# A graph attention layer: edge tiles taken two at a time, one PSUM sum and one addition per pair

## The reference, cut to what is computed

```python
xh = (x @ W).reshape(N, H, D)                       # N x 8 x 32
a_src, a_dst = einsum(xh, att_src), einsum(xh, att_dst)   # N x 8
e = leaky_relu(a_src[src] + a_dst[dst], 0.2)
m = segment_max(e, dst, N)
e = exp(e - m[dst])
denom = segment_sum(e, dst, N)
msg = xh[src] * (e / denom[dst])[:, :, None]
out = segment_sum(msg, dst, N) + bias               # then batch norm, + x
```

## Time and profile before

| | |
|---|---|
| median of 3 runs | 2181.05 us (2179.94 to 2183.12) |
| the profiled execution | 2179.96 us |
| its span, first to last instruction | 2178.0 us |
| busy: PE, PE weight loads | 1758.3 us (81%), 1227.8 us (56%) |
| busy: DVE, ACT, POOL | 1415.2 us (65%), 1108.1 us (51%), 1214.5 us (56%) |
| mean granted TensorE clock | 0.908 |
| edge gathers | 879, 838.9 us of POOL |

### The profile page before, as it was taken

The page is one execution under the profiler, slowest core; times in us unless marked ns, Lnnn a source line. Parts: engine busy times, 40 slices in busy tenths (PEclk is TensorE's granted clock), DMA queues, the critical chain, the costliest instruction groups (busy, mean ns, idle before and its releaser), DMA issues. The chain is left out here.

```text
span 2178.0 us, 37746 instructions
## 1 busy us (share of the span) xinstructions
PE 1758.3 (81%) x10860; PEld 1227.8 (56%) x10860; DVE 1415.2 (65%) x3855; ACT 1108.1 (51%) x2386; POOL 1214.5 (56%) x1142
## 2 busy tenths in 40 slices
PE   7567778678777687687776887788399999999997
PEld 5334445354444354454443444447179999999996
DVE  6745666567666566566665676589956666666664
ACT  4444655465556456455654565548644444444443
POOL 1465655566656556566655566642046666656653
PEclk9778988888989889889998899899699999999999
DMA  8543444443444344344533444426723333333322
GB/s 292 168 123 95 123 108 116 116 136 97 121 138 123 96 130 126 97 125 122 146 93 108 133 127 108 118 61 229 292 64 51 51 51 51 50 51 51 51 43 36
DMA packets 124147, 240.42 MB, mean 110 GB/s; under 512 B 25064, under 2 KB 82996, under 8 KB 122772
## 3 DMA queue, kind: packets, MB, share of 16 engines
q0 software_dynamic: 62800, 147.76, 28.7%
q1 hardware_dynamic: 51816, 80.51, 11.2%
q10 hardware_dynamic: 9340, 9.73, 1.3%
HBM read 195.47 MB, written 43.30 MB: 110 GB/s over the span
## 5 line engine op out<-in xcount | busy, mean ns | idle before, releaser
L1145 POOL DMA_INDIRECT gather_ring<-node_table,src_slot x879 | 838.9, 954 | 530.8 <-issue 238.8
L1273 PE MATMUL bank<-gather_ring,onehot 128*128 128x264 f32 x1758 | 622.6, 439 | 262.0 <-DVE gather_ring L1197 222.0
L1239 PE MATMUL bank<-ones 128*128 128x512 bf16 x1803 | 595.0, 412 | 50.9 <-ACT gather_ring L1315 31.6
L1273 PEld LDWEIGHTS bank<-gather_ring,onehot 128*128 128x128 f32 x1758 | 340.2, 214 | 496.6 <-DVE gather_ring L1197 320.2
L1169 DVE TENSOR_TENSOR acc<-acc,bank 128x264 f32 x879 | 370.9, 422 | 192.5 <-remote 98.7
L1197 DVE TENSOR_TENSOR gather_ring<-gather_ring,bank 128x256 f32<-128x256 f32 x879 | 361.6, 412 | 0.3 <-ACT bank L1314 0.3
L1314 ACT ACTIVATE bank<-zbuf 128x64 f32<-128x64 f32 x110 | 25.0, 228 | 615.2 <-DVE zbuf L1191 346.5
L2240 POOL DMA_INDIRECT out_rows<-y,token_idx x105 | 203.6, 1939 | 218.4 <-DMA out_rows<-y,token_idx 151.7
L1239 PEld LDWEIGHTS bank<-ones 128*128 128x128 bf16 x1803 | 180.5, 104 | 208.4 <-issue 81.1
L2148 PE MATMUL bank<-xe,w_hi 128*128 128x256 f16 (+1 forms) x1792 | 284.2, 267 | 3.8 <-DVE xe L2070 2.6
L2208 ACT ACTIVATE hid<-bank,cols 128x256 f32<-128x256 f32 (+1 forms) x448 | 210.6, 551 | 150.7 <-PE bank L2148 137.3
(11 more groups left out here) (323 smaller groups left out, 1932.7 us busy)
## 6 DMA issues: line engine op xcount, KB each, us to landing
stage<-in_L_ffn_W SPq DMA_DIRECT2D x16, 1024.0 KB
dst_row<-dst_rows SPq DMA_DIRECT2D x110, 128.0 KB
gather_ring<-node_table,src_slot POOLq DMA_INDIRECT x879
w_split<-w_out SPq DMA_DIRECT2D x32, 256.0 KB
w<-w_split SPq DMA_DIRECT2D x8, 1024.0 KB, 9.9
node_table<-acc ACTq DMA_DIRECT2D x24, 264.0 KB
r_ring<-in_x_lanes SPq DMA_DIRECT2D x7, 896.0 KB, 8.0
xt<-in_x_lanes SPq DMA_DIRECT2D x24, 256.0 KB
```

Source lines behind the costliest of these rows:

```text
L1145: e.indirect_dma_start(out=gather_ring[:, b % GB, j, :], out_offset=None, in_=node_table, in_offset=bass.IndirectOffsetOnAxis(ap=src_slot[ ...
L1239: e.matmul(to[:, :].rearrange("p (k n) -> p k n", k=2), halves[:, 0:P], halves.rearrange("p (a n) -> p a n", a=1).broadcast_to([P, 2, 2 * ...
L1273: e.matmul(bank[AGG[s % len(AGG)]][:, 0:ROW], onehot[:, b % OHB, j, :], gather_ring[:, b % GB, j, :], start=True, stop=True).then_inc(summ ...
```

## The change

An edge tile's rows are gathered once. The edge tiles are taken in couples (256 edges, 416 couples, CT), and a slot is a couple and a node tile: 464 slots, four per batch (SB), 116 batches. PE multiplies both halves of a couple into the same bank as one PSUM sum, with one post of `summed`, and DVE adds once per slot, two slots behind instead of three. A message covers both edge tiles and is written to a ring of its own, `message_ring`, of six slots, instead of in place; a couple that lies on a border is read twice out of the ring of gathered rows, at a place that a register gives. So the gathers, in 104 groups of eight (832), don't go in step with the batches: POOL waits on `messages` by a list of counts, and SP waits on the gathers by another and passes them on to DVE as `rows_landed`. The ring of `onehot` has two batches instead of three. In stage 1 the source lists are loaded as they lie and turned, and only the lists of destinations are gathered.

```diff
-        EB = 8
-        SLOTS = ceil_div(ET + NT - 1, EB) * EB
-        BATCHES = SLOTS // EB
-        USED = ET + NT - 1
+        COUPLE = 2
+        WIDE = COUPLE * P
+        CT = ceil_div(E, WIDE)
+        EB = 8
+        SB = EB // COUPLE
+        USED = CT + NT - 1
+        SLOTS = ceil_div(USED, SB) * SB
+        BATCHES = SLOTS // SB
...
-        OHB = 3
+        MR = 6
+        message_ring = early.take("message_ring", [P, MR, COUPLE, ROW])
+        OHB = 2
...
-        AGG, ADDS_BEHIND = (0, 1, 3, 4), 3
+        AGG, ADDS_BEHIND = (0, 1, 3, 4), 2
...
         def load_tiles(e, b):
-            _, values = nc.values_load_multi_w_load_instructions(
-                node_tile_row[0:1, b * EB:(b + 1) * EB], engines=[e.engine], min_val=0, max_val=NT,
-                skip_runtime_bounds_check_because=IN_RANGE)
-            tile_regs[e.engine, b] = values
+            if b % 2 == 0:
+                values = load_row_of(e, TILES_AT, b * SB, min(2, BATCHES - b) * SB, 0, NT)
+                tile_regs[e.engine, b], tile_regs[e.engine, b + 1] = values[0:SB], values[SB:]
...
         def pool_edges(e, batches):
-            for b in batches:
-                if b >= GB:
-                    e.wait_ge(summed, (b - GB + 1) * EB)
-                for j, s in enumerate(slots_in(b)):
+            for t in batches:
+                if t >= GB:
+                    if (t - GB) % SPANS_AT_ONCE == 0:
+                        at = t - GB
+                        spans = load_row_of(e, SPANS_AT, at, min(SPANS_AT_ONCE, TILE_BATCHES - GB - at), 1, USED)
+                    e.wait_ge(messages, spans[(t - GB) % SPANS_AT_ONCE])
+                    e.sem_inc(m_sems["passed"], 1)
+                for j, i in enumerate(tiles_of(t)):
                     e.indirect_dma_start(
-                        out=gather_ring[:, b % GB, j, :], out_offset=None, in_=node_table,
-                        in_offset=bass.IndirectOffsetOnAxis(ap=src_slot[:, s:s + 1], axis=0)
-                    ).then_inc(gathered[b % GB], 16)
+                        out=gather_ring[:, t % GB, j, :], out_offset=None, in_=node_table,
+                        in_offset=bass.IndirectOffsetOnAxis(ap=src_tile[:, i:i + 1], axis=0)
+                    ).then_inc(gathered[t % GB], 16)
...
+            def row_at(b, j):
+                return ring_rows[:, bass.ds((b * SB + j - tile_regs[e.engine, b][j]) % PLACES, 1), :, :]
+
             def score(b):
-                e.wait_ge(gathered[b % GB], 16 * (EB * (b // GB) + len(slots_in(b))))
+                e.wait_ge(rows_landed, GB * (b + 1))
...
-                vector_order.of(e.tensor_tensor(zbuf[:, 0, :, :], gather_ring[:, b % GB, :, D:ROW],
-                                                picked[:, b % 2, :, 0:HEADS], ALU.add))
+                for j in range(len(slots_in(b))):
+                    of = slice(COUPLE * j, COUPLE * (j + 1))
+                    vector_order.of(e.tensor_tensor(zbuf[:, 0, of, :],
+                                                    row_at(b, j)[:, :, :, D:ROW].rearrange("p a r h -> p (a r) h"),
+                                                    picked[:, b % 2, of, 0:HEADS], ALU.add))
...
             def message(b, j):
-                row = gather_ring[:, b % GB, j, 0:D].rearrange("p (h d) -> p h d", d=DH)
+                s = b * SB + j
                 if j == 0:
                     e.wait_ge(weighed, 2 * b + 1)
-                e.tensor_tensor(row, row, weights(b)[:, j, :].rearrange("p (h a) -> p h a", a=1)
-                                .broadcast_to([P, HEADS, DH]), ALU.mult).then_inc(messages, 1)
+                if s >= MR:
+                    e.wait_ge(summed, s - MR + 1)
+                e.tensor_tensor(message_ring[:, s % MR, :, 0:D].rearrange("p r (h d) -> p r h d", d=DH),
+                                row_at(b, j)[:, :, :, 0:D].rearrange("p a r (h d) -> p (a r) h d", d=DH),
+                                weights(b)[:, COUPLE * j:COUPLE * (j + 1), :].rearrange("p r (h a) -> p r h a", a=1)
+                                .broadcast_to([P, COUPLE, HEADS, DH]), ALU.mult).then_inc(messages, 1)
...
                 for j, s in enumerate(slots_in(b)):
-                    keep_clock(e, IDLE_PRODUCTS // 2 // EB, idle_bank)
+                    keep_clock(e, IDLE_PRODUCTS // 2 // SB, idle_bank)
                     e.wait_ge(messages, s + 1)
                     if s >= len(AGG):
                         e.wait_ge(added, s - len(AGG) + 1)
-                    e.matmul(bank[AGG[s % len(AGG)]][:, 0:ROW], onehot[:, b % OHB, j, :], gather_ring[:, b % GB, j, :],
-                             start=True, stop=True).then_inc(summed, 1)
+                    for r in range(COUPLE):
+                        made = e.matmul(bank[AGG[s % len(AGG)]][:, 0:ROW], onehot[:, b % OHB, COUPLE * j + r, :],
+                                        message_ring[:, s % MR, r, :], start=(r == 0), stop=(r == COUPLE - 1))
+                    made.then_inc(summed, 1)
...
                 e.activation(weights(b), zbuf[:, 1, :, :], ACT.Exp).then_inc(weighed, 1)
-                e.activation(gather_ring[:, b % GB, :, D:ROW], zbuf[:, 1, :, :], ACT.Exp).then_inc(weighed, 1)
+                if b:
+                    e.wait_ge(summed, (b + 1) * SB - MR)
+                for q, n in ring_parts(b):
+                    at = (b * SB + q) % MR
+                    made = e.activation(message_ring[:, at:at + n, :, D:ROW].rearrange("p q r h -> p (q r) h"),
+                                        zbuf[:, 1, COUPLE * q:COUPLE * (q + n), :], ACT.Exp)
+                made.then_inc(weighed, 1)
...
+            def landed(b):
+                if b % 2 == 0 and b >= GB:
+                    values = load_row_of(e, LANDED_AT, b * GB, min(2, BATCHES - b) * GB, 16 * EB,
+                                         16 * EB * ceil_div(TILE_BATCHES, GB))
+                    landed_regs[b], landed_regs[b + 1] = values[0:GB], values[GB:]
+                for q in range(GB):
+                    if b >= GB:
+                        e.wait_ge(gathered[q], landed_regs[b][q])
+                    elif q <= b:
+                        e.wait_ge(gathered[q], 16 * EB)
+                    e.sem_inc(rows_landed, 1)
...
             for b in range(BATCHES + 2):
+                if b < BATCHES:
+                    landed(b)
                 sync_weights(e, b)
```

More of the change, by code:

```diff
@@ L186, in build_gnn_moe @@
         s1 = Region(early_b)
+        TILES_AT, SPANS_AT, LANDED_AT = 0, 32, 64
+        PLACES = GB * SB
+        TILE_BATCHES = ceil_div(ET, EB)
+        assert PLACES & (PLACES - 1) == 0 and GB * BATCHES <= SLOTS_UP and SLOTS_UP // SB >= TILE_BATCHES
+        assert SB == GB
         iota_slot = s1.take("iota_slot", [P, SLOTS_UP])
         above = s1.take("above", [P, SLOTS_UP])
[L189 to L192, removed]
+        raw_src = s1.take("raw_src", [P, TILE_GROUPS, P], I32)
+        raw_src_f = s1.take("raw_src_f", [P, TILE_GROUPS, P])
+        raw_idx = s1.take("raw_idx", [P, 4, WIDE], I32)
+        raw_f = s1.take("raw_f", [P, 2, WIDE])
+        raw_row = s1.take("raw_row", [P, SLOT_GROUPS, WIDE], U8)
+        row_up = s1.take("row_up", [P, WIDE])
         x_ring = 8
@@ L503, in scalar_stage1 @@
                     store(pair_of(NT - 1))
-                g, which = divmod(n - LISTS_AT - 17, 2)
-                if n >= LISTS_AT + 17 and which == 0 and g < SLOT_GROUPS:
+                g, which = divmod(n - KEPT_AT - 2, 2)
+                if n >= KEPT_AT + 2 and which == 0 and g < SLOT_GROUPS:
                     e.wait_ge(rows_clamped, g + 1)
@@ new lines, in vector_slot_step @@
+                for h in range(2):
+                    hs = slice(h * HALF_SLOTS, (h + 1) * HALF_SLOTS)
+                    vector_order.of(e.tensor_copy(slot_table[landed, hs], bank[5 + h][landed, 0:HALF_SLOTS]))
+            if n == LISTS_AT + 4 + SLOT_GROUPS:
+                e.wait_ge(vector_order.sem, vector_order.n)
+                ends = slot_table[landed, 0:BATCHES * SB].rearrange("p (b q) -> p b q", q=SB)[:, :, SB - 1]
+                e.tensor_single_scalar(last_batch[landed, :], ends, 2, ALU.arith_shift_right).then_inc(slot_keys_made, 1)
@@ L694, in tensor_stage1 @@
                     e.wait_ge(w_folded, 2)
-                    e.wait_ge(slots_counted, SLOT_GROUPS)
+                    e.wait_ge(src_kept, TILE_GROUPS)
+                    e.wait_ge(slots_counted, SLOT_GROUPS + 1)
+                    e.matmul(bank[7][:, P:P + SLOT_GROUPS * PER_GROUP], ones[:, :],
+                             end_keys[:, :, :].rearrange("p g j -> p (g j)"), start=True, stop=True).then_inc(slots_summed, 1)
                     for g in range(SLOT_GROUPS):
@@ L1203, in messages_and_adds @@
                     if s >= ADDS_BEHIND:
-                        add(*divmod(s - ADDS_BEHIND, EB))
-                    if j == EB // 2 - 1:
+                        add(*divmod(s - ADDS_BEHIND, SB))
+                    if j == 1 and b + 1 < BATCHES:
```

(4 more changed lines are left out.)

238 lines of the change are left out of this document (150 added, 88 removed).

## The result

The changed kernel takes 2343.25 us (2334.94 to 2350.3, 4 runs) against 2182.09 before on the same chip: ratio 1.0735, interval 1.0693 to 1.0777. It is 7.35% slower, where a gain of 1% was forecast. On another chip, on which the kernel before takes 1903 us instead of 2182, the same changed kernel is 3.2% faster (1842.66 us, ratio 0.9684, interval 0.9668 to 0.97); on a second one with 1904 us three close variants of it gave the same (0.966 to 0.968). Both results have to be explained.

What follows compares the result with a forecast made beforehand. The edge stage was taken as bound by PE's late posts during gathers and POOL's waits on them. Groups 1280 plus extra batches 25 make 1305 against 1319, -14; start -6; sum -20, 2161, said 2160 us, own range 2080 to 2200.

Steps and rivals of the forecast that it cites:

- What bounds the kernel: Edge stage, 1319.1 us: PE's posts arriving late while gathers are in flight, and POOL's wait on them, set the period.
- the burst at 461.13: Edge-stage timeline: PE's late posts arrive all at once, about 2 us after the last gather's issue began.
- DVE's costs: Edge stage: message 0.60 us, addition 0.33, score's first operation some 0.4 more per batch; DVE some 100 us less in all.
- rival D: Edge stage: DVE's messages hold up the gathers' issue, +150, 2330 us; chance 0.04.
- Stage 1: Stage before the edge stage: turns other lists, its end unchanged; no change, bounds +-2 us.
- The cycle: Edge stage: POOL issues two groups in a row as a rule; 25.6 us for two, 1280 us for 100 groups.
- then one batch on DVE, 4.2: Edge stage, per two groups: after the posts arrive DVE needs 4.2 us for one batch, then POOL is released.
- 20.0: Edge stage, per two groups: 16 gathers at 1.25 us take 20.0 us.
- the 1.4: Edge stage, per two groups: time until the posts arrive after the gathers, 1.5 us, added as 1.4.
- A: Edge stage: POOL's pauses let PE's posts through, fewer pauses starve them; slower, 2270 us (2200 to 2320); chance 0.38.
- B: Edge stage: five posts always fit the free window, POOL never waits and is the bound; about -290, 1890 us; chance 0.08.
- C's lockstep: Edge stage: DVE releases POOL once per batch, as now; -13 to -25, 2168 us (2150 to 2185); chance 0.14.

Runs made afterwards that it cites:

- n3: Kernel before without the gathers after the fourth batch and DVE's waits on them, on a chip with late posts: 1783.89 us, 0.8136 of before.
- l4: Changed kernel with POOL waiting by constants, for the slot's sum instead of its message, where posts are late: 2168.20 us, 0.9925 of before.
- l2: Changed kernel with POOL waiting on messages by constants, without register loads and extra post, where posts are late: 2287.03 us, 1.0455 of before.
- n2: Changed kernel with POOL waiting for the slot's sum instead of its message, register wait and post kept, posts late: 2225.45 us, 1.016 of before.
- l1: Changed kernel unaltered, on a chip where posts are late: 2326.23 us, 1.0625 of before.
- n1: Same kernel as l4, run again on another chip with late posts: 2164.63 us, 0.987 of before.
- m1: Kernel before, with PE's eighth product of a batch waiting until the group in flight has landed, posts late: 2290.05 us.
- m4: As m1, with POOL's wait also made an instruction of its own with a post behind it: 2337.77 us.
- e1: Kernel before with POOL's wait an instruction of its own and a post behind it, on a chip without late posts: 1903.66 us, 1.0001.
- n4: As l4, with the additions three slots behind instead of two, where posts are late: 2139.87 us, 0.974 of before.
- e4: Changed kernel with the additions three slots behind instead of two, on a chip without late posts: 1839.49 us, 0.9664 of before.
- c2: Changed kernel with constant waits on POOL and additions four slots behind, on a chip without late posts: 1838.65 us, 0.9659 of before.

## Why the prediction was wrong

**What bounds the kernel**: right for the chip of the profile. PE's late posts and POOL's pauses set the time, and n3 shows that gathers in flight make the posts late. One reading of the rows is off: the burst at 461.13 comes 2 us after the last gather's issue ended, not after it began (458.17).

**DVE's costs**: the message was right (0.59 us from its start to the next, 680 ns busy; 0.60 taken), the addition too. The score's four operations cost 1.06 instead of 0.26 us, 0.8 more and not 0.4. DVE had 86 us less to do, for "some 100". (415 x 0.157 is 65 us, not 64.) None of it decided. A gather takes 954 ns as before: rival D fell.

**Stage 1**: "no change, bounds +-2 us" was wrong; the first gather starts at 78.2 instead of 85.4.

**The cycle**: the step that failed is "POOL will issue two groups in a row as a rule ... after which POOL is released. 25.6 us for two groups". Most groups stayed single (62 pauses after single ones, 18 after pairs), and a pair took 19.7 us of gathers and 11.7 of pause, 31.4. The premise was "DVE posts; I have found no late post of DVE's ... So it has one more batch of slack than before". But a message stands on DVE behind a reduce and additions that wait for late posts. The wait moved from the burst to the work that the burst sets free. In one word that is worth some 100 us: l4 against l2 119, and n2's 1.016 against 1.0625. In the pair the term that was too small is "then one batch on DVE, 4.2": the sum had DVE through the first batch in the free window and standing at the second one's picks. It stood at an addition in 13 of the 18 pairs, and from the end of its last stand to POOL's gather it took 7.1 us on average. The sum's other end was too dear: 20.0 holds the last gather whole, and the 1.4 is counted from that gather's start; by its own rows it is 19.02 + 1.54 + 4.2 = 24.8 for 25.6.

**What was left out**: POOL's wait as an instruction of its own with a post behind it, after which the gather starts 0.78 us from the release instead of 0.26. The order's rows showed a wait on the gather and the diff showed the post; neither had a price in my sum. Measured: 39 us (l1 to l2) and 61 (n1 to n2), with the register loads, 48 (m1 to m4) without them, so the register isn't needed for it; nothing where POOL doesn't pause (e1).

**The rivals**: A had the sign, but not the size (2270; 2343 lies outside 2200 to 2320), and only part of the reason: pairs rose from 6 to 18, but single groups carry most of the loss. Their pauses are 62 x (4.77 - 2.46) = 143 us longer; what a pair's pause costs beyond two single ones of before is 18 x (11.0 - 4.92) = 109 us now and 6 x (8.7 - 4.92) = 23 before, 86 more, in which the later release has its part too. No run parts the two within a pair. B, given 0.08, is what happens without late posts, at 1843 instead of 1890. Against it I had "no stretch of the trace has posts on time with over eight gathers in a row": true of that trace, which is one chip's. C's lockstep stayed, with a longer period.

## What to carry to other kernels

When a wait is moved to another semaphore, follow the new poster back on its engine to the instruction that it stands behind, and ask which late event that one waits for: an earlier point in the data flow can release later than one behind it. Price the wait's own form (on a register, with a post behind it) for each time that the engine really pauses. And before a design is chosen by its waits, time the kernel on more than one chip: the change costs 7% on one and gains 3% on another. The version that beats the kernel before where posts are late is n4 (0.974), with constants that fit these edge lists only; without late posts n4 was not run, the nearest are e4 and c2 (0.966).

## What the hardware showed unexpectedly

The same kernel before took 1903 and 1904 us on two chips and 2182 to 2193 on at least two others (the record names two, one of them at 2193 both times, and doesn't name the chip of the first runs). The difference is that PE's semaphore posts are seen 0.01 us (median) after the modelled end of the product on the first, and up to some 13 us late in the same kernel on the others while gathers are in flight, mostly until the last one has landed. DVE's, ACT's and POOL's own work takes the same time on both: a message 412 ns here and 414 in e1, a one-hot 387 and 390, a gather 954 and 956. Without gathers the posts are in time on such a chip too. Why one chip shows it and another doesn't stays open, and whether it is the posting of PE alone: the traces with late posts also lack semaphore records (727 of the 879 sums' are there in the kernel before, all 879 in e1).
